# Reordering the prologue of layer 0 in a two-layer attention kernel

## The reference

```python
# layer 0
qs = (x @ Wq.T).reshape(b, s, H, 2, F)          # H = 8, F = 16
ks_ = (x @ Wk.T).reshape(b, s, H, 2, F)
vs = (x @ Wv.T).reshape(b, s, H, DH)            # DH = 32
scores = einsum('bqhif,bkhif->ibhqk', qs, ks_) * scale
atts = softmax(scores, axis=-1)
att = atts[0] - diff_weight * atts[1]
o = einsum('bhqk,bkhe->bqhe', att, vs)          # then RMS norm, Wo, bo
g = silu(top-2-of-8 gated low-rank product of xn)
x = x + s * g
# layer 1: attention over the batch's 8 entries' tokens with distance
# embeddings (16 heads of 64), gate from sqrt((xn cos)^2 + (xn sin)^2)
x = x + s * g
```

## Time and profile before

| | us |
|---|---|
| median of three runs | 1212.56 (1211.91 to 1213.89) |
| the profiled execution, its time | 1215.19 |
| its span, first to last instruction | 1213.1 |
| PE busy in the span | 1157.1 |
| DVE busy | 899.0 |
| ACT busy | 677.9 |
| POOL busy | 575.6 |

### The profile page before, as it was taken

How to read it: one execution, slowest core, us unless ns; L and a number is a source line. 1 busy time by engine, 2 the same in 40 slices (tenths; PEclk the granted TensorE clock), 3 DMA queues, 4 the chain that set the end, 5 groups by cost and what they waited for, 6 DMA issues and landing times. The chain is left out here.

```text
span 1213.1 us, 34870 instructions
## 1 busy us (share of the span) xinstructions
PE 1157.1 (95%) x14293; PEld 752.8 (62%) x14293; DVE 899.0 (74%) x1989; ACT 677.9 (56%) x1302; POOL 575.6 (47%) x603
## 2 busy tenths in 40 slices
PE   7899999999999999999948999999999999999997
PEld 6433444444444444443337787888878787887976
DVE  6776887878788787878255777779686777869766
ACT  3456677677767677666633444535344444535443
POOL 2057486777868677686642314223231423224131
PEclk9578999999999999999988999999999999999999
DMA  8614445462525445353230001010101001010100
GB/s 234 148 28 115 106 115 149 93 167 50 147 72 141 123 115 132 80 138 100 71 108 18 4 20 37 4 53 4 53 4 54 3 9 48 4 53 4 36 4 19
DMA packets 57998, 86.80 MB, mean 72 GB/s; under 512 B 8304, under 2 KB 38256, under 8 KB 57840
## 3 DMA queue, kind: packets, MB, share of 16 engines
q1 hardware_dynamic: 57840, 84.58, 26.6%
HBM read 50.40 MB, written 33.55 MB: 69 GB/s over the span
## 5 line engine op out<-in xcount | busy, mean ns | idle before, releaser
L1091 DVE TENSOR_REDUCE negmax<-s_bank 128x1 f32<-128x512 f32 x512 | 330.4, 679 | 75.9 <-PE s_bank L760 75.2
L1278 POOL TENSOR_TENSOR room<-room 128x512 f32<-128x512 f32 x248 | 310.1, 1285 | 127.7 <-ACT room L913 127.7
L913 ACT ACTIVATE room<-t_bank 128x512 f32<-128x512 f32 x512 | 283.9, 600 | 78.0 <-PE t_bank L770 74.4
L770 PE MATMUL t_bank<-qst,kst 50*128 50x512 f32 x512 | 202.9, 473 | 5.8 <-ACT room L913 5.7
L760 PE MATMUL s_bank<-kst,qst 48*128 48x512 f32 x512 | 196.1, 475 | 6.9 <-DVE negmax L1091 6.1
L770 PEld LDWEIGHTS t_bank<-qst,kst 50*128 50x128 f32 x512 | 82.1, 189 | 100.6 <-ACT room L913 62.9
L2028 POOL TENSOR_TENSOR win<-rt,apart 128x512 f32<-128x512 f32 x32 | 41.9, 1332 | 212.5 <-DVE rt L1834 212.5
L1566 PE MATMUL pr<-xt_h,win_h 128*128 128x512 f32 x256 | 105.8, 413 | 0.0
L2015 POOL TENSOR_TENSOR ex<-ex,rc 128x256 f32<-128x256 f32 x64 | 41.8, 653 | 129.2 <-DVE rc L1862 129.2
L1566 PE MATMUL pr<-xt_h,win_l 128*128 128x512 f32 x256 | 100.5, 393 | 0.0
L1566 PE MATMUL pr<-xt_l,win_h 128*128 128x512 f32 x256 | 100.5, 392 | 0.0
(11 more groups left out here) (317 smaller groups left out, 2570.2 us busy)
## 6 DMA issues: line engine op xcount, KB each, us to landing
park<-qk_h SPq DMA_DIRECT2D x128, 128.0 KB, 2.5
qst<-park SPq DMA_DIRECT2D x64, 192.0 KB, 3.3
kst<-park SPq DMA_DIRECT2D x64, 192.0 KB, 4.3
park<-qk_l SPq DMA_DIRECT2D x64, 128.0 KB, 2.4
room<-in_x SPq DMA_DIRECT2D x8, 512.0 KB, 5.2
xr<-in_x SPq DMA_DIRECT2D x8, 512.0 KB, 6.1
room<-x SPq DMA_DIRECT2D x8, 512.0 KB, 3.9
out<-so SPq DMA_DIRECT2D x32, 128.0 KB, 1.7
```

Source lines behind the costliest of these rows:

```text
L770: pe.matmul(t_bank[w % 2][:, :], kst[slot][rows, j, c * P:(c + 1) * P], qst[slot][rows, j, :], start=True, stop=True).then_inc(m.t_done, 1)
L913: act.activation(probs[:, c, j, :], t_bank[w % 2][:, :], ACT.Exp, scale=SCALE0).then_inc(m.exp_done, 1)
L1091: dve.tensor_reduce(negmax[:, i_par, 2 * odd + j, c:c + 1], s_bank[n % S_BANKS][:, :], X, ALU.max, negate=True).then_inc(m.max_done, 1)
L1278: add = pool.tensor_tensor(sums[:, pair, h, :], probs[:, 2 * pair, h, :], probs[:, 2 * pair + 1, h, :], ALU.add)
```

## The change

- `PROJ` 3 moves behind the 22 leading scores on TensorE, into `a_bank` in place of `misc`.
- Its two copies move into the first batch: ScalarE's to (half 0, unit 4), VectorE's to (0, 6). The first value product, which writes `a_bank`, waits for them.
- `low_waves` on VectorE moves from in front of the first batch to (0, 8).
- `GK` and `BETA` move from behind `PROJ` 2 to in front of `V` 0.
- One product that nothing reads (128 rows, 512 columns, into `t_bank[0]`) follows each of the first 16 leading scores; for that TensorE waits until `PROJ` 1 is drained from this bank. After each stands a separate semaphore increment.

```diff
-        first_banks = (a_bank, d_bank, misc, t_bank[0], t_bank[1], a_bank, d_bank, t_bank[1], misc)
+        first_banks = (a_bank, d_bank, misc, t_bank[0], t_bank[1], a_bank, d_bank, t_bank[1], a_bank)
...
-            def warm_up(n):
+            def warm_up(n, bank):
 
                 for _ in range(n):
-                    pe.matmul(s_bank[0][:, :], kst[0][:, 0, 0:P], kst[0][:, 1, :], start=True, stop=True)
+                    pe.matmul(bank[:, :], kst[0][:, 0, 0:P], kst[0][:, 1, :], start=True, stop=True)
                 stand_alone(pe, m.warm)
...
                 if c == 0:
                     wait(pe, m.a_evac, y)
+                if isinstance(b, int) and (b, hf, c) == (0, 0, 0):
+                    pe.wait_ge(m.qk_low, 4)
...
-            warm_up(16)
+            warm_up(16, s_bank[0])
             first_tokens()
-            warm_up(5)
+            warm_up(5, s_bank[0])
             for n in range(KC, len(FIRST_JOBS) - 2):
+                if FIRST_JOBS[n] == ("V", 0, 0):
+                    pe.wait_ge(*done(2))
+                    job("GK", 0, 0, misc)
+                    job("BETA", 0, 0, misc)
                 first_job(n)
-            pe.wait_ge(*done(2))
-            job("GK", 0, 0, misc)
-            job("BETA", 0, 0, misc)
+            pe.wait_ge(*done(3))
             for n in range(FIRST_LEAD):
                 score_max(n, n % UNITS, n // UNITS, n // UNITS)
+                if n < UNITS:
+                    warm_up(1, t_bank[0])
                 if n == UNITS:
                     first_job(len(FIRST_JOBS) - 2)
-                    pe.wait_ge(shared.g_ok, 2)
-                    first_job(len(FIRST_JOBS) - 1)
+            first_job(len(FIRST_JOBS) - 1)
+            pe.wait_ge(shared.g_ok, 2)
             for n in range(len(FIRST_JOBS) - 1):
                 pe.wait_ge(*done(n))
             pe.wait_ge(m.fold, 5)
-            prev = FIRST_JOBS[-1]
+            prev = FIRST_JOBS[-2]
...
-            for n, (kind, i, k) in enumerate(FIRST_JOBS):
+            for n, (kind, i, k) in enumerate(FIRST_JOBS[:-1]):
                 side(kind, i, k, first_banks[n])
...
+                        if first and (hf, w) == (0, 4):
+                            side(*FIRST_JOBS[-1], first_banks[-1])
...
-            side("PROJ", 3, 0, first_banks[8])
-            shared.low_waves(dve)
...
+                        if first and (hf, w) == (0, 6):
+                            side(*FIRST_JOBS[-1], first_banks[-1])
+                        if first and (hf, w) == (0, 8):
+                            shared.low_waves(dve)
```

## The result

The changed kernel is slower: 1222.83 us median of seven runs (1217.30 to 1225.87) against 1213.89 us (1211.17 to 1216.76) for the one before. The ratio is 1.0064, with a 95% interval of 1.0045 to 1.0084. The forecast was 1208.6 with a range of 1202 to 1215. The profiled execution took 1222.83 us with a span of 1220.7, 7.6 above the one before.

What follows compares the result with a forecast made beforehand. TensorE was taken to bound whole batches without slack, so start gains reach the end; VectorE bounds the leading scores. Terms 4.5 + 2.5 - 1.9 - 0.5 - 0.6 = 4.0 us, so 1212.56 - 4.0 = 1208.6, range 1202 to 1215.

Steps and rivals of the forecast that it cites:

- The unread products: Among the first 16 scores: pairs take 0.85 us at half clock, 0.43 at full; cost 0.5 us, bounds 0 and 4.0.
- The clock: Before the leading scores: `V` and `PROJ` 2 should bring it up near the first score, with two scores at half clock.
- Rival C: Clock stays at half through all 16 scores, exponential 1 gains only 3.0: 2.9 us slower, 1215.5; chance 0.13.
- Start of the scores: `GK` and `BETA` ahead of `V` 0: first score at 30.7 instead of 28.8, cost 1.9 us, bounds 0 and 5.4.
- T to exponential 1: From T, the 17th maximum's end: exponential 1 at T + 6.7 against T + 11.25, gain 4.5 us (3.0 at half clock).
- Exponential 1 to exponential 12: First half of batch 0: 13.1 us instead of 15.6, VectorE the bound at full clock; gain 2.5, bounds 0 and 4.5.
- What is late next: SyncE's queue: later `park_parts(3)` delays `place_max(1)`, landing near T + 22, which unit 16 needs; cost 0.6 us, bounds 0 and 2.
- The two later half-clock stretches: Stretches of 10.2 and 6.8 us at 1.2 GHz after the first of 41.0; left as they are, no term in the sum.

Runs made afterwards that it cites:

- e1: The changed kernel without the 16 unread products; ratio to the kernel before 0.9972, median 1213.12 against 1215.82 us.
- e2: The kernel before with only the 16 unread products and the wait for `PROJ` 1 added; ratio 1.0105, median 1229.3 against 1215.82 us.
- e4: The changed kernel with the same unread products of 128 rows, two behind every two scores; ratio to the kernel before 0.9991.
- e6: The changed kernel with the separate semaphore increment only after the last unread product; ratio to the kernel before 1.0088, median 1226.46 us.
- e9: e4 with `GK` and `BETA` back behind `PROJ` 2; ratio to the kernel before 1.0017, median 1.7 us above it.
- e10: e8 with further unread products behind scores 16 and 19 and in batch 0, to hold the clock; ratio to the kernel before 0.9980.
- e12: e10 with the copies of `PROJ` 3 at units 1 and 2 and `low_waves` ahead of the first batch; ratio to the kernel before 0.9957, median 1208.91 us.
- e7: The kernel before with only `PROJ` 3 moved behind the leading scores and its copies in the first batch; ratio 0.9973.
- e11: e3 with the copies of `PROJ` 3 at units 1 and 2 instead of 4 and 6; ratio to the kernel before 0.9975.
- e3: e1 with `GK` and `BETA` behind `PROJ` 2 again; ratio to the kernel before 0.9955, 1210.71 against 1215.82 us.
- e5: e4 with unread products of 48 rows in the half of the array that neighbours leave free; ratio to the kernel before 0.9988.
- e8: e4 with the `GK` and `BETA` products mixed one at a time between large products and 12 more unread ones; ratio to the kernel before 1.0007.

## Why the prediction was wrong, point by point

**The unread products: the step that failed.** "A score and an unread product together take 2 x 0.43 = 0.85 us at half clock ... at full clock 0.43." They took 1.45 and 0.86. I had priced both by their columns, from rows in which neighbours are alike: products of 128 rows next to each other, and scores whose rows lie in alternate halves. No row of before showed a 48-row and a 128-row product in turn, and I gave the change between them no bound. With 0.86 over VectorE's 0.60 even at full clock, the term of 0.5 us (bound 4.0) became 10. e1, e2, e4, e6 and the rows of e9 show that it is this change that costs, not the products, and not the increments.

**The clock.** Right was that it would come up before the scores (29.6). Wrong was that it would stay: it fell at 36.4 among the pairs, so ten of the sixteen took 1.45. TensorE was busy for all of the 6.80 us before that fall. It had been so before 24.3 in the kernel before as well (3.40 of 3.40, with products of 16 columns), where the prediction spoke of idling; before 75.5 it was busy for 2.03 of 3.40 us. Rival C, the slower side, had the sign and much of the clock, but with its price of 0.25 us for each pair it reached only 2.9 us of loss; the range ended at 1215.

**Start of the scores.** Cost 1.9 forecast. The first maximum was 1.8 later than before, of which 1.0 lies in the execution's own late start (first low part stored from 18.44, not 17.42); e1 shows 2.6 for another execution. The mechanism was right (the first small product at 19.18, `V` behind `BETA`, half clock), the size within its bounds.

**T to exponential 1.** 4.5 at full clock, 3.0 at half: measured 3.1 at half clock (T + 8.1 against T + 11.2), and the full-clock place, T + 6.7, is that of e10 (T + 6.4) and e12 (T + 6.65). Right.

**Exponential 1 to exponential 12.** Gain 2.5 forecast. Measured 16.2 us (59.78 to 76.01) against 15.0; the prediction's 15.6 for before counted one unit too far (unit 12 is the first of the four at 66.17). So a loss of 1.2, just outside the lower bound of 0, and all of it ran at half clock. `low_waves` isn't the cause: e7, which has it ahead of the batch, took the same 16.2 (48.67 to 64.90). Half of the loss, 0.6, is VectorE's copy of `PROJ` 3, which the lower bound took to be hidden behind TensorE at half clock. At (0, 6) it stands in front of `ml`, and TensorE's next job in `misc` waits for `ml`:

```profile
71.12 1.11 PE L677 MATMUL misc<-ident,room 128*128 128x128 f32 x4 [0.54 <-DVE ml L1115]
```

In e11, with this copy at unit 2, the wait is gone. The other half is the clock of the kernel before, which was up from 65.3 on the earlier trace rows, just before its exponential 12. At full clock the stretch took 13.2 (e10) and 13.0 (e12) against the 13.1 forecast: the price was right, its clock was wrong. `low_waves` cost more than alone, as the prediction said. It took 2.70 us for its two halves with GpSimd at work, as much as 3.29 in e11, against 1.28 alone. Twice the 1.69 of `wo_l` is 3.4, so that row was a fair bound.

**What is late next.** The chain through SyncE was named, and priced at 0.6 because I took about 2 us for the landing. TensorE stood 0.55 us for it in the changed kernel:

```profile
80.56 0.79 PE L770 MATMUL t_bank<-qst,kst 50*128 50x512 f32 x1 [0.55 <-DMA qst<-ml]
```

The size was right by luck: the issue came at T + 23.2 and not at T + 19, the landing took until 4.5 us after its end, and unit 16 itself came at T + 29.7 and not at T + 22 to T + 24. It isn't what ate the gain either: e3 stood 0.13 us for it and e11 not at all, and both have exponential 16 where the changed kernel has it. What did is the 1.2 above and the clock: from exponential 12 to 16 the changed kernel took 5.4 us at half clock (76.01 to 81.39), the kernel before 3.1 (66.17 to 69.26) at full.

**The two later half-clock stretches.** Left as they were in the sum. They were gone in the changed kernel, and from T to the last mark it gained 6.1 us, where the terms 4.5 + 2.5 - 0.6 make 6.4: the right sum for partly wrong reasons, since unit 16 had nothing of it. The profiled executions of the changed kernel, e3, e5 and e7, in which the clock held in batch 0 once it had come up, all have this mark at T + 71.8 or 71.9, as has e1 with a short fall of 3.4 us at 78.4; e4 and e8, where it fell again for 6.8 us about 100, have T + 74.3 and T + 73.4. So the moved steps do win 6 us over the profiled execution of before, of which some 3 are in the first half (the mark of half 1 is 3.1 sooner) and the rest hangs on where the clock falls. Over all executions the moves are worth less, 3 to 5 us (e1, e3, e7). Why the clock comes up at about T + 32.5 in the changed kernel, e3 and e7 and came up at T + 25.4 before, and why it then holds, stays open; it was only set beside the traces, not tested.

## What to carry to other kernels

Price an inserted product by its neighbours, not by its columns. If it shares only a part of its rows with the product before it and after it (48 of 128 here), its weight load and its neighbour's come into the open. Neighbours with the same 128 rows, or with no rows in common, didn't show this. Grouping such products two and two can make the same work free (e4), if the clock is up; at half clock it still cost 5 us (e9). An unread product that is to hold the clock has to fit into the time the bound engine leaves at the lower clock too, or it becomes the bound just when it is needed. And follow an early win by marks through the whole next stage: here it was there at unit 1, gone at unit 16 and back, doubled, at the end of the batch, as the clock fell at other places.

## What the runs showed that was not expected

- A change between 48-row and 128-row products, from start to start: 0.43 us for 512 columns at 2.4 GHz and 0.72 at 1.2 GHz, against 0.23 and 0.43 between products of 128 rows.
- Two scores in different halves of the array, next to each other, took 0.72 us together at 1.2 GHz, as long as one between products of 128 rows.
- With pairs of 48-row products the clock fell at 36.5, with pairs of 128 rows at the same places it held until 43.8, and with single products of 128 rows it fell at 36.4. These are single executions.
- The placed maxima, 8 KB, were waited for until 4.3 to 4.5 us after the end of their issue, behind a load of 512 KB in the same queue.
- Two subtractions of `low_waves` took 1.28 us alone and 2.48, 2.70 and 3.29 beside GpSimd's sums.
- The trace lists each of the 24 small float32 products of `GK` and `BETA` as two instructions (x32 and x16); the text ahead counts 48 products.
